# Probabilities applied in two runs of four steps, with eight places for their transposes

## The chip, the cores and the metric

The kernel runs on one core of a Trainium2 chip. The metric is the device time of one execution in microseconds (us). The kernel before took 1561.91 us, the median of 3 runs (1559.69 to 1562.31).

## What is computed

64 graphs of 128 nodes with 512 features go through two layers. The first is attention with 16 heads of 32 features; the adjacency matrix of the graph, taken twice, is added to the scores. The second is a graph convolution with one expert out of four for each graph, and a normalization over all the rows of an expert. Cut to the part that the change touches:

```python
h = maximum(layernorm(x), 0)
q, k, v = heads(h @ Wq.T), heads(h @ Wk.T), heads(h @ Wv.T)
a = einsum('bhnd,bhmd->bhnm', q, k) * 512 ** -0.5 + (adj + adj)
p = softmax(a)                                  # rows that are all zero give 0
o = einsum('bhnm,bhmd->bhnd', p, v)
x = x + merge(o) @ Wo.T
# then the expert layer on x
```

## The kernel before, in words

`attention_layer` works on pairs of graphs, 32 pairs in all. A pair has eight steps (`STEPS`): steps 0 to 3 are the four groups of four heads of its first graph, steps 4 to 7 those of its second. One step is a chain over all the engines, and each link is a letter in the order strings:

- `S` (TensorE, line 420): four score matmuls, one for each head, into one of two PSUM places.
- `L` (VectorE, 356 and 361): scaling and adjacency into `logits`, then the row maxima. `B` (364) tells all-zero rows, `R` (369, 372) makes the factor of each row.
- `E` (ScalarE, 301): four exponentials. `P` (GpSimd, 268): the probabilities times the row factor.
- `T` (TensorE, 427): four transposes of 128x128 into one of two PSUM places (`probT_ps`). `C` (ScalarE, 308) copies them to `probT` in SBUF.
- `W` (TensorE, 436): the probabilities are applied. It is a matmul for each of four heads, with 32 columns of `v` as weights and 128 columns of `probT` moving; each writes 32 partitions of `o_ps` (128 partitions, one 128-column place for each group of heads). In the trace each is two load and matmul pairs, so a `W` is eight loads and eight matmuls.

Beside the chain run the projections, each a sum of products of split operands by `exact_product` (line 43): `Q` 0 to 3 (24 matmuls each, the projections to queries and keys), `V` 0 and 1 (12 each), `O` 0 and 1 (12 each, the output projection), and `H` 0 and 1 (line 477, four transposes of the input). ScalarE and VectorE take each result out of PSUM as a high and a low part (`Q` at 319 and 387, `H` at 333 and 405, `O` at 312 and 377); ScalarE alone copies `V` (325). `X` on VectorE (381) adds the residual.

The order is written out by hand, one string for each engine, with one line for each step of the loop over pairs; each engine works its tokens strictly in this order. A prime means the pair before. Each token waits on semaphores, which count steps. The ones that matter here:

- `T` waits for the scaled probabilities of its step and for the copy `C` two steps before. `C` waits for the `W` that last read its place of `probT`.
- `W` waits for the copy of its step; `W0` and `W4` wait also for the copy of `v` and for the split of `o_ps` as it was before.
- `O` on ScalarE waits for the fourth `W` of its graph. `V` on ScalarE waits likewise, since it overwrites `v`.
- `Q2` on TensorE waits for the copy `V1'` (they share a bank).
- `K0` and `K1` on SyncE stack the split queries and keys for a graph's four steps: twelve DMAs each (line 249), issued one after the other. `K0` waits for the split of `Q3`, and `K1'` comes behind it on the queue with a store and a load in between. `S0` waits for `K0`'s data and `S4` for `K1'`'s; ScalarE's `Q0`, which overwrites what the copies read, waits for both.

The orders of ScalarE and GpSimd, which the change leaves alone:

```python
    ACT_ORDER = """H1' C6' E0
                   C7' E1
                   C0 Q0 O1' E2
                   V1' Q1 C1 E3
                   Q2 C2 E4
                   Q3 C3 E5
                   C4 A0 O0 E6
                   A1 V0 C5 H0 E7"""
    POOL_ORDER = "P7' D1' P0 P1 P2 P3 G P4 D0 P5 P6"
```

`probT` is also one of three tensors through which the raw weights are loaded at the start (`raw_weights`, 2048 values in each partition).

Of the kernel before, what the change touches and what calls it, by code (L numbers as in the profile page):

```python
# [25 lines left out]
ACT = mybir.ActivationFunctionType  # L26
# [6 lines left out]
def wait(engine, semaphore, value):  # L33

    if not isinstance(value, int) or value > 0:
        engine.wait_ge(semaphore, value)
# [31 lines left out]
def attention_layer(nc, ctx, sem, ident, x, adj, weights, x1_dram, expert_w, shared):  # L68
    w_hi, w_raw, w_raw_loaded, ew_hi_ready, ew_split, x1_in, x1_loaded = shared
    B, N, D = x.shape  # L70
    PAIRS = B // 2
    KC = D // 128
    R = 4
    C = HEADS // R
    HD = D // HEADS
    STEPS = 2 * C
    SCALE = float(D) ** -0.5
    STACKS = 16 * 3 * R

    def sb(name, shape, dt=F32):  # L80
        return ctx.enter_context(nc.sbuf_tensor(name, shape, dt))

    def ps(name, shape):
        return ctx.enter_context(nc.psum_tensor(name, shape, F32))
# [10 lines left out]
    v = sb("v", [N, 2, D])  # L95
    logits = sb("logits", [N, 4, R, N])
    prob = sb("prob", [N, 4, R, N])
    probT = sb("probT", [N, 4, R, N])
    o_hi = sb("o_hi", [128, C, N], F32R)
    o_lo = sb("o_lo", [128, C, N], F32R)  # L100
    x_res = sb("x_res", [N, 2, D])
# [18 lines left out]
    probT_ps = ps("probT_ps", [N, 2, R, N])  # L120
    o_ps = ps("o_ps", [128, C, N])
# [15 lines left out]
    transposed, probT_ready, applied = sem("transposed"), sem("probT_ready"), sem("applied")  # L137
# [8 lines left out]

    PE_ORDER = """S0 W5' T6' H1' O0'
                  S1 T7' W6' Q0  # L150
                  S2 T0 W7' Q1
                  S3 T1 W0 Q2
                  S4 W1 T2 Q3
                  S5 T3 W2 O1'
                  S6 T4 W3 V0
                  S7 T5 W4 H0 V1"""

    ACT_ORDER = """H1' C6' E0
                   C7' E1
# [31 lines left out]
    def tokens(engine, order, i):  # L191

        for t in (START.get((engine, i), order) if isinstance(i, int) else order).split():
            pair = 0 if t[0] in "UF" else i + (AHEAD[engine].get(t[0], 0) - t.endswith("'"))
            if not isinstance(pair, int) or 0 <= pair < PAIRS:
                yield t[0], int(t[1:].strip("'") or 0), pair

    def raw_weights(n):

        return (logits, prob, probT)[n % 3][:].rearrange("p k r n -> p k (r n)")  # L200

    def exists(pair):
        return not isinstance(pair, int) or pair < PAIRS
# [1 line left out]
    def run(engine, body):  # L205
        for i in (-2, -1, 0, 1):
            body(i)
        with engine.Fori(2, PAIRS - 2) as i:
            body(i)
        for i in (PAIRS - 2, PAIRS - 1, PAIRS):  # L210
            body(i)

    with nc.Block() as block:
# [70 lines left out]
        @block.scalar  # L284
        def _(act):
            def body(i):
                for token, k, j in tokens("act", ACT_ORDER, i):
                    slot = k % 4
                    if token == "U":
                        act.wait_ge(w_loaded[k], 16)  # L290
                        nc.scalar.activation(w_hi[:, k], raw_weights(k), ACT.Copy).then_inc(w_hi_ready, 1)
                    elif token == "F":
                        act.wait_ge(qk_projected, 4 * PAIRS)
                        act.wait_ge(v_projected, 2 * PAIRS)
                        act.wait_ge(w_raw_loaded[k], 16)
                        nc.scalar.activation(w_hi[:, k], w_raw[:, k].bitcast(F32), ACT.Copy).then_inc(ew_hi_ready, 1)
                    elif token == "E":
                        wait(act, neg_max_ready, STEPS * j + k + 1)
                        wait(act, transposed, STEPS * j + k - 3)
                        for r in range(R):  # L300
                            last = nc.scalar.activation(prob[:, slot, r], logits[:, slot, r], ACT.Exp,  # L301
                                                        bias=neg_max[:, slot, r:r + 1],
                                                        accum_out=row_sum[:, slot, r:r + 1])
                        last.then_inc(exp_done, 1)
                    elif token == "C":
                        wait(act, transposed, STEPS * j + k + 1)
                        wait(act, applied, STEPS * j + k - 3)
                        nc.scalar.activation(probT[:, slot], probT_ps[:, k % 2], ACT.Copy).then_inc(probT_ready, 1)  # L308
                    elif token == "O":
                        wait(act, applied, STEPS * j + C * (k + 1))  # L310
                        wait(act, o_projected, 2 * j + k)
                        nc.scalar.activation(o_hi[:], o_ps[:], ACT.Copy).then_inc(o_hi_ready, 1)
                    elif token == "Q":
                        wait(act, qk_projected, 4 * j + k + 1)
                        if k == 0:
                            for g in range(2):
                                wait(act, stacked[g], STACKS * j)
                        t, c = (Q_HI, K_HI)[k // 2], 2 * (k % 2)
                        nc.scalar.activation(qk[:, t, :, c:c + 2].rearrange("p g c n -> p c g n"),  # L319
                                             bank[:, Q_BANK[k]].rearrange("p (c g n) -> p c g n", c=2, g=2),  # L320
                                             ACT.Copy).then_inc(qk_hi_ready, 1)
                    elif token == "V":
                        wait(act, v_projected, 2 * j + k + 1)
                        wait(act, applied, STEPS * (j - 1) + C * (k + 1))
                        nc.scalar.activation(v[:, k], bank[:, V_BANK[k]], ACT.Copy).then_inc(v_copied, 1)
                    elif token == "A":
                        wait(act, shift_ready, j + 1)
                        wait(act, h_transposed, 2 * (j - 1) + k + 1)
                        nc.scalar.activation(h[:, k], x_in[:, k], ACT.Relu, bias=shift[:, k:k + 1],
                                             scale=rstd[:, k:k + 1]).then_inc(h_ready, 1)  # L330
                    elif token == "H":
                        wait(act, h_transposed, 2 * j + k + 1)
                        nc.scalar.activation(hT_hi[:, :, k], bank[:, H_BANK[k]].rearrange("p (c n) -> p c n", n=N),
                                             ACT.Copy).then_inc(hT_hi_ready, 1)

            run(act, body)

        @block.vector
# [72 lines left out]
        def _(pe):  # L411
            def body(i):
                for token, k, j in tokens("pe", PE_ORDER, i):
                    g, c, slot = k // C, k % C, k % 4
                    if token == "S":
                        if c == 0:
                            wait(pe, stacked[g], STACKS * (j + 1))
                        wait(pe, logits_ready, STEPS * j + k - 1)
                        for r in range(R):
                            last = nc.tensor.matmul(scores_ps[:, k % 2, r], stack[:, g, r, 0, c], stack[:, g, r, 1, c],  # L420
                                                    start=True, stop=True)
                        last.then_inc(scored, 1)
                    elif token == "T":
                        wait(pe, normed, STEPS * j + k + 1)
                        wait(pe, probT_ready, STEPS * j + k - 1)
                        for r in range(R):
                            last = nc.tensor.transpose(probT_ps[:, k % 2, r], prob[:, slot, r], ident[:])  # L427
                        last.then_inc(transposed, 1)
                    elif token == "W":
# [3 lines left out]
                            wait(pe, o_split, 2 * j + g)  # L433
                        for r in range(R):
                            f = HD * (R * c + r)
                            last = nc.tensor.matmul(o_ps[HD * r:HD * r + HD, c], v[:, g, f:f + HD], probT[:, slot, r],  # L436
                                                    start=True, stop=True)
                        last.then_inc(applied, 1)
                    elif token == "O":
# [11 lines left out]
                    elif token == "Q":  # L451
# [5 lines left out]
                        for half in range(2):  # L457
                            m = 128 * (2 * (k % 2) + half)
                            last = exact_product(nc, bank[:, Q_BANK[k], 256 * half:256 * half + 256],
                                                 [w_hi[:, k // 2, kc, m:m + 128] for kc in range(KC)],  # L460
                                                 [w_lo[:, k // 2, kc, m:m + 128] for kc in range(KC)],
                                                 [hT_hi[:, kc] for kc in range(KC)], [hT_lo[:, kc] for kc in range(KC)])
# [9 lines left out]
                    elif token == "H":  # L472
# [3 lines left out]
                        for kc in range(KC):  # L476
                            last = nc.tensor.transpose(bank[:, H_BANK[k], 128 * kc:128 * kc + 128],
                                                       h[:, k, 128 * kc:128 * kc + 128], ident[:])
                        last.then_inc(h_transposed, 1)

            keep_clock_up(nc, pe, bank[:, 0, 0:128], ident, 40)
            run(pe, body)


def expert_layer(nc, ctx, sem, ident, x1_dram, adj, router_w, router_b, gamma, beta, out_dram, y, shared):
# [92 lines left out]

    PE_ORDER = "Z0 Z1 J P0 P1 Z2 P2 Z3 P3 M"
    ACT_ORDER = "A2' A3' Z0 P0 A0 A1 Z1 P1 Z2 P2 Z3 P3"  # L580
# [66 lines left out]
    with nc.Block() as block:  # L647
# [255 lines left out]
        def _(pe):  # L903
            def body(i, stays):
                for token, g, group in tokens("pe", PE_ORDER, i):
                    n = G * group + g
# [146 lines left out]
```

## Time and profile before

| | |
|---|---|
| median of 3 runs | 1561.91 us |
| the profiled execution | 1559.98 us, span 1557.9 us |
| mean granted clock of TensorE | 0.977 of full speed |
| TensorE matmul busy | 1480.9 us (95%) |
| VectorE busy | 1137.4 us (73%) |
| ScalarE busy | 999.9 us (64%) |
| GpSimd busy | 444.7 us (29%) |
| attention layer | from the start to about 1140 us of the span |

Matmuls are pipelined: a matmul's record is some 0.28 us long, and the next one starts long before it has ended. So what a block of matmuls costs is read from the starts, from the first matmul of one block to the first or second matmul of the next, not from the durations. In the timeline, neighbours of one kind are merged to one row with a count.

### The profile page before, as it was taken

The page shows a single profiled execution, that of the slowest core. Times are in us where ns is not written, and L with a number is a line of the kernel's source. Part 1 is how long each engine was busy: PE and PEld are TensorE (multiplying, and loading weights), DVE is VectorE, ACT ScalarE, POOL GpSimd, SP SyncE. Part 2 cuts the span into 40 slices and gives each one's busy share as a digit, 9 for nine tenths or more (in the row PEclk, how much of TensorE's full clock was granted, in tenths as well). Part 3 has the DMA queues.
Part 4 walks back from the last instruction along what each step waited for, and adds up shares of the span by engine and source line. Part 5 has one row for each costly group of instructions (what it writes and reads, how often), then busy time and mean ns, then how long its engine had stood idle before and what let it go on. Part 6 is the DMA issues. An engine that isn't in the chain of part 4 may idle for free. (4 is left out here: it accounts for less than half of the span.)

```text
span 1557.9 us, 39084 instructions
## 1 busy us (share of the span) xinstructions
PE 1480.9 (95%) x11474; PEld 1264.9 (81%) x11475; DVE 1137.4 (73%) x2641; ACT 999.9 (64%) x3145; POOL 444.7 (29%) x529
## 2 busy tenths in 40 slices
PE   7999999999999999999999999999969999998885
PEld 6888888888888888888888888888757777777775
DVE  4777777777777777777777777777676667676685
ACT  4667666766676677666666766676644454453495
POOL 0223222322223222222232222222223343443200
PEclk9999999999999999999999999999879999999997
DMA  5965556666655566665555666654524332220798
GB/s 180 254 145 142 125 125 144 150 151 152 144 131 125 128 148 147 155 148 145 126 125 135 148 150 151 149 139 112 136 89 135 123 124 87 67 68 14 268 406 327
DMA packets 142135, 230.37 MB, mean 148 GB/s; under 512 B 17666, under 2 KB 34050, under 8 KB 142082
## 3 DMA queue, kind: packets, MB, share of 16 engines
q1 hardware_dynamic: 133634, 212.95, 52.7%
q10 hardware_dynamic: 8448, 16.78, 2.8%
q8 instruction: 25, 0.41, 0.1%
q14 instruction: 28, 0.23, 0.0%
HBM read 89.15 MB, written 39.85 MB: 83 GB/s over the span
## 5 line engine op out<-in xcount | busy, mean ns | idle before, releaser
L268 POOL TENSOR_TENSOR prob<-prob,norm 128x512 f32<-128x512 f32 x256 | 266.3, 1040 | 789.3 <-DVE norm L372 789.3
L301 ACT ACTIVATE prob<-logits,neg_max 128x128 f32<-128x128 f32 x1024 | 398.1, 394 | 69.7 <-DVE neg_max L361 69.6
L43 PE MATMUL bank<-hT_hi,w_hi 128*128 128x256 f32 x1024 | 303.1, 296 | 2.5 <-DVE hT_lo L405 2.2
L43 PE MATMUL bank<-hT_lo,w_hi 128*128 128x256 f32 x1024 | 290.7, 284 | 0.0
L43 PE MATMUL bank<-hT_hi,w_lo 128*128 128x256 f32 x1024 | 290.6, 284 | 0.0
L356 DVE SCALAR_TENSOR_TENSOR logits<-scores_ps,adj 128x512 f32<-128x512 f32 x256 | 176.7, 690 | 134.1 <-PE scores_ps L420 133.6
L308 ACT ACTIVATE probT<-probT_ps 128x512 f32<-128x512 f32 x256 | 152.7, 596 | 143.2 <-PE probT_ps L427 143.2
L43 PEld LDWEIGHTS bank<-hT_hi,w_hi 128*128 128x128 f32 x1024 | 196.7, 192 | 21.2 <-issue 19.5
L43 PEld LDWEIGHTS bank<-hT_lo,w_hi 128*128 128x128 f32 x1024 | 197.3, 193 | 0.0
L43 PEld LDWEIGHTS bank<-hT_hi,w_lo 128*128 128x128 f32 x1024 | 196.9, 192 | 0.0
L301 ACT ACTIVATION_READ_ACCUMULATOR prob<-logits,neg_max 128x1 f32 x1024 | 195.7, 191 | 0.0
L361 DVE TENSOR_REDUCE neg_max<-logits 128x4 f32<-128x512 f32 x256 | 175.7, 686 | 8.7
L364 DVE TENSOR_REDUCE abs_max<-logits 128x4 f32<-128x512 f32 x256 | 173.0, 676 | 0.0
L427 PE MATMUL probT_ps<-ident,prob 128*128 128x128 f32 x1024 | 163.6, 283 | 4.5 <-POOL prob L268 4.3
L420 PEld LDWEIGHTS scores_ps<-stack 96*128 96x128 f32 x1024 | 146.5, 193 | 16.4 <-DMA stack<-qk 5.6
L420 PE MATMUL scores_ps<-stack 96*128 96x128 f32 x1024 | 145.4, 265 | 4.7 <-DMA stack<-qk 4.7
L43 PE MATMUL out_ps<-w_hi,z_hi 128*128 x256 | 107.1, 418 | 20.6 <-issue 12.4
L750 ACT ACTIVATE z_hi<-z_ps 128x512 fp32r<-128x512 f32 x64 | 38.1, 598 | 137.4 <-PE out_ps L43 133.4
L427 PEld LDWEIGHTS probT_ps<-ident,prob 128*128 128x128 f32 x1024 | 108.6, 142 | 18.3 <-issue 12.7
L436 PE MATMUL o_ps<-probT,v 128*32 128x128 f32 x2048 | 109.8, 286 | 0.8 <-ACT probT L308 0.3
L387 DVE TENSOR_TENSOR qk<-bank,qk 128x512 fp32r<-128x512 f32 x128 | 87.8, 686 | 30.9 <-ACT qk L319 30.9
L319 ACT ACTIVATE qk<-bank 128x512 fp32r<-128x512 f32 x128 | 76.4, 597 | 52.4 <-PE bank L43 49.5
(138 smaller groups left out, 2921.5 us busy)
## 6 DMA issues: line engine op xcount, KB each, us to landing
stack<-qk SPq DMA_DIRECT2D x768, 128.0 KB, 2.5
x_in<-in_x SPq DMA_DIRECT2D x32, 512.0 KB, 4.7
x_res<-in_x SPq DMA_DIRECT2D x64, 256.0 KB, 2.9
x_dram<-x_res SPq DMA_DIRECT2D x64, 256.0 KB, 3.0
x_in<-x_dram SPq DMA_DIRECT2D x32, 512.0 KB, 3.7
y<-outs ACTq DMA_DIRECT2D x16, 1024.0 KB, 11.8
w_hi<-x_dram SPq DMA_DIRECT2D x8, 1024.0 KB, 17.9
out_dram<-outs SPq DMA_DIRECT2D x24, 256.0 KB, 2.0
```

What stands on the lines that cost most here:

```text
L43: last = nc.tensor.matmul(out, a, b, start=(n == 0), stop=(n == len(terms) - 1))
L268: nc.gpsimd.tensor_tensor(prob[:, slot], prob[:, slot], norm[:, slot].unsqueeze(2).to_broadcast([N, R, N]), ALU.mult).then_inc(normed, 1)
L301: last = nc.scalar.activation(prob[:, slot, r], logits[:, slot, r], ACT.Exp, bias=neg_max[:, slot, r:r + 1], accum_out=row_sum[:, slot, r: ...
L308: nc.scalar.activation(probT[:, slot], probT_ps[:, k % 2], ACT.Copy).then_inc(probT_ready, 1)
L319: nc.scalar.activation(qk[:, t, :, c:c + 2].rearrange("p g c n -> p c g n"), bank[:, Q_BANK[k]].rearrange("p (c g n) -> p c g n", c=2, g=2 ...
L356: nc.vector.scalar_tensor_tensor(out=logits[:, slot], in0=scores_ps[:, k % 2], scalar=SCALE, in1=adj2[:, k // C].unsqueeze(1).to_broadcast ...
L361: nc.vector.tensor_reduce(neg_max[:, slot], logits[:, slot], X, ALU.max, negate=True).then_inc(neg_max_ready, 1)
L364: nc.vector.tensor_reduce(abs_max[:, slot], logits[:, slot], X, ALU.max, apply_absolute_value=True).then_inc(abs_max_ready, 1)
L387: nc.vector.tensor_tensor(qk[:, lo, :, c:c + 2].rearrange("p g c n -> p c g n"), bank[:, Q_BANK[k]].rearrange("p (c g n) -> p c g n", c=2, ...
L420: last = nc.tensor.matmul(scores_ps[:, k % 2, r], stack[:, g, r, 0, c], stack[:, g, r, 1, c], start=True, stop=True)
L427: last = nc.tensor.transpose(probT_ps[:, k % 2, r], prob[:, slot, r], ident[:])
L436: last = nc.tensor.matmul(o_ps[HD * r:HD * r + HD, c], v[:, g, f:f + HD], probT[:, slot, r], start=True, stop=True)
```

## The change

The eight `W` tokens of a pair stood alone, one in each line of TensorE's order. Now four stand one behind the other in two places: `W0` to `W3` behind `T4`, and `W4'` to `W7'` of the pair before behind `T0`. The transposes wait longer before they are read, so `probT` has eight places in place of four, and the copy `C` waits for the `W` of eight steps before.

```diff
+    PROBT_SLOTS = 8
...
-    probT = sb("probT", [N, 4, R, N])
+    probT = sb("probT", [N, PROBT_SLOTS, R, N])
...
-    PE_ORDER = """S0 W5' T6' H1' O0'
-                  S1 T7' W6' Q0
-                  S2 T0 W7' Q1
-                  S3 T1 W0 Q2
-                  S4 W1 T2 Q3
-                  S5 T3 W2 O1'
-                  S6 T4 W3 V0
-                  S7 T5 W4 H0 V1"""
+    PE_ORDER = """S0 T6' H1' O0'
+                  S1 T7' Q0
+                  S2 T0 W4' W5' W6' W7' Q1
+                  S3 T1 Q2
+                  S4 T2 Q3
+                  S5 T3 O1'
+                  S6 T4 W0 W1 W2 W3 V0
+                  S7 T5 H0 V1"""
...
-        return (logits, prob, probT)[n % 3][:].rearrange("p k r n -> p k (r n)")
+        return (logits, prob, probT)[n % 3][:, 0:4].rearrange("p k r n -> p k (r n)")
...
                         wait(act, transposed, STEPS * j + k + 1)
-                        wait(act, applied, STEPS * j + k - 3)
-                        nc.scalar.activation(probT[:, slot], probT_ps[:, k % 2], ACT.Copy).then_inc(probT_ready, 1)
+                        wait(act, applied, STEPS * j + k - PROBT_SLOTS + 1)
+                        nc.scalar.activation(probT[:, k % PROBT_SLOTS], probT_ps[:, k % 2], ACT.Copy).then_inc(probT_ready, 1)
...
-                            last = nc.tensor.matmul(o_ps[HD * r:HD * r + HD, c], v[:, g, f:f + HD], probT[:, slot, r],
+                            last = nc.tensor.matmul(o_ps[HD * r:HD * r + HD, c], v[:, g, f:f + HD], probT[:, k % PROBT_SLOTS, r],
```

## Rows read from the trace of the kernel before

**Rows 1.** Windows: the middle pairs, the last pair; busy us of each engine, clock.
```profile
71.60:1106.00 1034.40, 1034.09 (x8397) 891.16 (x8398) 787.17 (x1760) 718.37 (x2517) 295.59 (x359) 1.00 0.60 141
1106.00:1145.00 39.00, 30.53 (x209) 22.40 (x207) 25.71 (x49) 24.19 (x80) 9.67 (x10) 0.82 0.36 106
```

**Rows 2.** Waits of TensorE's matmuls, 71.6 to 1106 us: total, times, longest.
```profile
PE scores_ps L420 <- DMA stack<-qk: 1.5, 1, 1.5
PE bank L43 <- ACT v L325: 0.3, 1, 0.3
```

**Rows 3.** Timeline of TensorE, three steps: start us, us, what, count.
```profile
503.11 0.56 PE L420 MATMUL scores_ps<-stack 96*128 96x128 f32 x4
...
503.96 0.66 PE L427 MATMUL probT_ps<-ident,prob 128*128 128x128 f32 x4
...
504.57 0.28 PE L43 MATMUL bank<-hT_lo,w_hi 128*128 128x256 f32 x1
...
520.24 0.56 PE L420 MATMUL scores_ps<-stack 96*128 96x128 f32 x4
520.72 0.43 PE L436 MATMUL o_ps<-probT,v 128*32 128x128 f32 x8
521.08 0.66 PE L427 MATMUL probT_ps<-ident,prob 128*128 128x128 f32 x4
521.58 0.60 PE L477 MATMUL bank<-ident,x_in 128*128 128x128 f32 x4
...
522.25 0.39 PE L43 MATMUL bank<-w_lo,o_hi 128*128 128x512 f32 x1
...
524.77 0.56 PE L420 MATMUL scores_ps<-stack 96*128 96x128 f32 x4
525.16 0.62 PE L427 MATMUL probT_ps<-ident,prob 128*128 128x128 f32 x4
525.72 0.43 PE L436 MATMUL o_ps<-probT,v 128*32 128x128 f32 x8
526.07 0.38 PE L43 MATMUL bank<-hT_hi,w_hi 128*128 128x256 f32 x1
526.30 0.28 PE L43 MATMUL bank<-hT_lo,w_hi 128*128 128x256 f32 x1
526.41 0.28 PE L43 MATMUL bank<-hT_hi,w_lo 128*128 128x256 f32 x1
```

**Rows 4.** Timeline: the weight loads of the `W` at 525.72.
```profile
525.72 0.16 PEld L436 LDWEIGHTS o_ps<-probT,v 128*32 128x32 f32 x8 [0.17 <-issue]
```

**Rows 5.** Timeline of TensorE: a block of small matmuls in the expert layer.
```profile
1201.28 0.95 PE L931 MATMUL router_ps<-rw,mean_h 128*1 128x4 f32 x32
```

**Rows 6.** Timeline: GpSimd's `P1` and TensorE's `T1`.
```profile
531.50 1.04 POOL L268 TENSOR_TENSOR prob<-prob,norm 128x512 f32<-128x512 f32 x1 [5.14 <-DVE norm L372]
...
533.71 0.62 PE L427 MATMUL probT_ps<-ident,prob 128*128 128x128 f32 x4
```

**Rows 7.** Timeline of SyncE's queue: issues of `K0`, then of `K1'`.
```profile
508.97 7.67 SPq L249 DMA_DIRECT2D stack<-qk  x12
...
518.44 7.67 SPq L249 DMA_DIRECT2D stack<-qk  x12
```

**Rows 8.** Line 249: issue to landing, of the second twelve of Rows 7.
```profile
DMA to landing us min/median/max: 3.9/4.1/4.2
```

**Rows 9.** The same, of all of line 249 from 100 to 1100 us.
```profile
DMA to landing us min/median/max: 2.3/2.5/5.6
```

**Rows 10.** Timeline: ScalarE's `Q0` and `V1'`, TensorE's `Q2`.
```profile
530.59 0.59 ACT L319 ACTIVATE qk<-bank 128x512 fp32r<-128x512 f32 x1
...
533.09 0.59 ACT L325 ACTIVATE v<-bank 128x512 f32<-128x512 f32 x1
...
534.62 0.38 PE L43 MATMUL bank<-hT_hi,w_hi 128*128 128x256 f32 x1
```

**Rows 11.** Waits of ScalarE, 71.6 to 1106 us: total, times, longest.
```profile
ACT qk L319 <- DMA stack<-qk: 2.5, 3, 1.2
```

## The prediction

> **What bounds the kernel now.** I read the page's busy shares and the slices of the granted clock first: TensorE is at 95% of the span, the next engine at 73%. Busy shares of pipelined matmuls flatter the engine, so I then asked for windows. From the first `S` of the second pair (71.6 us) to the first `S` of the last (1106.0 us) TensorE's matmuls are busy for 1034.09 of 1034.40 us, with the clock at 1.00, its level of 2.4 GHz [rows 1]. That is 30 pairs (8397 matmuls at 280 a pair), 34.48 us each. In the same stretch the table of waits gives the matmuls two waits for others, 1.8 us together [rows 2]. VectorE is busy for 76% of it and ScalarE for 69%. So in these 30 pairs TensorE's own order sets the time, and what is saved on it is saved in full until some other chain comes up.
>
> The third view is TensorE's timeline, which shows where its time goes without idling. Ahead of a `W` and behind it there are holes between starts. In a block of ordinary matmuls 0.11 us lies between starts (526.30 to 526.41). The eight matmuls of a `W` start close together (0.43 us from first start to last end, for records of 0.28 us), yet the transposes before take 0.56 us until the `W` starts, and the next block starts 0.35 us behind the `W`'s start [rows 3]. Its loads are over after 0.16 us, and the load side sat idle for 0.17 us before them for nothing that the profile names ("issue") [rows 4]. I read this as TensorE running empty each time it goes between matmuls over 128 columns of weights and matmuls over 32.
>
> **What a `W` costs now.** I measure from the first matmul of `S` to the second matmul of the projection (the first starts early and waits for its load). All from [rows 3]:
> - `S T W Q`: 526.30 - 524.77 = 1.53 us.
> - `S W T Q`: 504.57 - 503.11 = 1.46 us.
> - Without a `W`: `S` to `T` is 0.39 us (524.77 to 525.16); `T` to the second matmul of `Q` is 504.57 - 503.96 = 0.61 us, less 0.04, since a `T` behind a `W` runs 0.66 us and one behind an `S` 0.62 us. Sum 0.96 us.
> - So a `W` between `T` and a projection costs 0.57 us, and one between `S` and `T` 0.50 us.
> - `S W T H O`: 522.25 - 520.24 = 2.01 us; without the `W` 0.39 + (0.50 - 0.04) + 0.67 = 1.52 us, so 0.49 us.
>
> The starts are rounded to 0.01 us, so I take 0.56 for the five `W` ahead of a projection (`W6'`, `W7'`, `W0`, `W2`, `W3`) and 0.50 for the three between `S` or `T` and transposes (`W5'`, `W1`, `W4`). Sum for a pair: 2.80 + 1.50 = 4.30 us.
>
> **What it costs afterwards.** Two runs of four, each between `T` and a projection. The first `W` of each pays 0.56 us, which holds both emptyings. The other six pay what a `W` adds inside such a run, m. No two `W` stand together in the steady part, so m is bounded:
> - From below: a block of 32 load and matmul pairs of four columns runs 0.95 us from first start to last end with records of 0.17 us, so 0.025 us a pair [rows 5]; eight of them are 0.20 us.
> - From above: a `W` that empties the engine again for itself, 0.35 us from its start to that of the next block (525.72 to 526.07) [rows 3].
> - My value: the eight matmuls are two passes of four that run side by side. Four transposes with the same 128 moving columns take 0.62 us with records of 0.28 us, so 0.11 us each [rows 3]; two passes are 0.22 us. The single `W` supports it: 0.43 - 0.28 = 0.15 us from its first start to its last, of which a part is the first load.
>
> Then a pair's `W` cost 2 x 0.56 + 6 x 0.22 = 2.44 us, and 4.30 - 2.44 = 1.86 us are saved. Over 30 pairs: 55.8 us. With m = 0.20 it is 59 us; with m = 0.35 it is 1.08 us a pair, 32 us.
>
> **What the freed time runs into.** The step chains. `T1` and `T5` are the tight ones: `P1` ends at 532.54 and `T1` starts at 533.71, 1.17 us of cover [rows 6]. But between `S2`, on which `P1` hangs through VectorE's order, and `T1` three more `W` come in (+0.66 us), so this cover grows, and that of `T5` with it. All other transposes have no such `L` between their exponentials and their row factor and a cover over twice as long; they lose at most two `W`, 1.06 us. ScalarE's `O0` and `O1'` wait for the fourth `W`, which now ends 0.66 us later behind its `T`; but one copy and another operation (0.6 us and more each) stand ahead of them in ScalarE's order, so this costs 0.1 us there at most. The eight places cost nothing: `C` waits for a `W` that is long done, as before.
>
> The chain that does come closer is that of the stacking copies. `K0` starts when `Q3` is split, and `K0` and `K1'` keep SyncE's queue until 526.11; the last DMA is issued at 525.5 and takes 4.1 us to land [rows 7, 8], so it is there at 529.6. ScalarE's `Q0` starts at 530.59 [rows 10]: 1.0 us of cover. Between `Q3` and `Q0`'s place TensorE saves `W2`, `W4`, `W5'`, `W6'` (0.56 + 0.50 + 0.50 + 0.56) and gets three more in line 7 (0.66): 1.46 us. So `Q0` on ScalarE will wait some 0.5 us for the landing, in nearly each pair. Behind it in the order come `O1'`, `E2` and `V1'`, and TensorE's `Q2` waits for `V1'`: it ends at 533.68, `Q2` starts at 534.62, 0.94 us of cover [rows 10], and `Q2` itself moves by + 0.66 - 0.56 = 0.10 us. Cover together 1.0 + 1.04 against 1.46: 0.6 us are left, and TensorE doesn't feel it. In three of the 30 pairs `Q0` waited for the landing already, 2.5 us together [rows 11], and once the wait got through to TensorE [rows 2]. There the cover at `Q0` is nil: 3 x (1.46 - 1.04) + 2.5 = 3.8 us come back as stalls. I take 4 us, between nothing and, were it so in each pair with the longest landing (5.6 us [rows 9], 1.5 more than here), 30 x 0.9 = 27 us.
>
> **The ends.** The last pair and its tail have TensorE busy for 30.53 of 39.00 us, at a mean clock of 0.82 [rows 1]: it waits for the step chain there, which the change doesn't shorten. Only the first lines gain, 1 us or so. In the first pair the same: two `W` less ahead of `Q3` bring `K0` forward by up to 1 us. I take 2 us for both, of 0 to 3. The expert layer isn't touched.
>
> **Sum.** -55.8 + 4 - 2 = -53.8 us. Against the profiled execution (span 1557.9, in all 1559.98 us) that is 1506.2 us; the median of the runs lies 1.9 us above it, so 1508 us.
>
> **A rule that speaks against it.** In the trace 32 load and matmul pairs run at 0.025 us each [rows 5] and the eight matmuls of a `W` start within 0.15 us, 0.02 us each [rows 3]. The Trainium skill, "TensorE: Matmul & The Clock Gate", section "Wait — 56ns, not 53.3ns?", has the sequencer spend about 62 ns on each matmul when hardware decode is off, and names that as the bound for short matmuls. By that rule a `W` in a run would take at least 0.50 us by the page's figure, and the sum would be 1562 - 30 x 0.18 - 2 = 1555 us. These rows contradict it, unless a queue filled beforehand fed them; the rival "the run starves" is that doubt, with its price from rows.
>
> A second rule: the loads of a `W` are all issued while its own first matmuls run (loads over at 0.16 us, matmuls at 0.43 us [rows 3, 4]). The same page, section "The mechanism" of its Part 3, says that a load overlaps with matmuls in flight only when it goes to another row group, and all of these use all rows. By it each pass would wait out the one before. The trace of a single `W` disagrees, but has one change of weights only; the rival "no overlap" is this rule's.
>
> **The rivals.**
> - *Each `W` still empties the engine*, because each has its own waits and weights: m = 0.35, 1.08 us saved a pair, -32 - 2 and no stalls of the copies: 1528 us. For it: "issue" idling isn't explained by a semaphore. Against: the scores also wait token by token, and start 0.39 us ahead of the transposes with no hole [rows 3].
> - *The copies take over*: landing gets slower as the same DMAs fall in less time, and the chain `K0`, `K1'`, `Q0`, `V1'`, `Q2` sets the pair. At half of the upper bound above, 14 us, come back on top of my 4: 1522 us. For it: already three waits [rows 11] and a landing that varies from 2.3 to 5.6 us [rows 9].
> - *No overlap of loads in a run*: a pass takes its load (0.11 us) and its matmuls (0.15 us), m = 0.52; 4.30 - 1.12 - 3.12 = 0.06 us a pair: about 1560 us, no change.
> - *Slower: the run starves.* 64 loads and matmuls stand in a row. If those beyond what is queued come only as fast as the projections show them, 0.11 us a pair [rows 3], a `W` takes 0.88 us: 1.12 + 6 x 0.88 = 6.40 us a pair against 4.30, +63 us: 1625 us. It decides from m = (4.30 - 1.12) / 6 = 0.53 us, 0.066 us for a load and its matmul. For it: nothing shows that projections aren't fed at just that rate. Against: the 32 pairs at 0.025 us [rows 5].
>
> **How the numbers follow.** Forecast 0.66; copies take over 0.16; each `W` empties 0.09; no overlap 0.04; starves 0.04; 0.01 for something else. The first three are faster by far more than 0.2% (3 us, about what a measurement of this kernel tells from no change): faster 0.92 with part of the fourth, same 0.03, slower 0.05. The forecast's own range is 1502 (m = 0.20, no stalls) to 1517 (m = 0.26). The range reaches on to the copies' and to the emptying case: 1501 to 1530.
>
> **What would show it.** In the profile after: a pair of 32.6 to 32.8 us; a merged row of 32 matmuls of line 436, 1.1 us long (0.28 + 0.15 + 3 x 0.22), longer in the rivals (1.5 emptying, 2.0 no overlap, 3.1 starving); "issue" idling ahead of line 436 down to a quarter; ScalarE's `Q0` waiting for the stacking DMAs in most pairs, 0.3 to 1 us each; TensorE's waits for `V` a few us in all; `T1` and `T5` with more cover than before. I am wrong if TensorE shows waits of over 10 us for others between 71.6 us and the last pair, or if the run of 32 is over 1.4 us long.

## The result and the profile after

The changed kernel took 1517.62 us, the median of 4 runs (1513.03 to 1519.4), against 1561.11 us for the one before on the same chip: a ratio of 0.9717, with a 95% interval from 0.9692 to 0.9743. The forecast was 1508 us, with a range from 1501 to 1530. The profiled execution took 1519.4 us, its span was 1517.6 us. On a second chip the changed kernel took 1507.55 us; what lies between the two is taken up below.

First the run of four `W` in TensorE's timeline, in a stretch where nothing disturbs it. The columns are start, duration, what, and count; PEld is the side that loads weights.

```profile
744.28 0.56 PE L421 MATMUL scores_ps<-stack 96*128 96x128 f32 x4
744.68 0.62 PE L428 MATMUL probT_ps<-ident,prob 128*128 128x128 f32 x4
745.24 1.08 PE L437 MATMUL o_ps<-probT,v 128*32 128x128 f32 x32
...
749.62 0.62 PE L428 MATMUL probT_ps<-ident,prob 128*128 128x128 f32 x4
750.00 0.36 PE L43 MATMUL bank<-hT_hi,w_hi 128*128 128x256 f32 x1
...
776.97 0.56 PE L421 MATMUL scores_ps<-stack 96*128 96x128 f32 x4
```

```profile
745.23 0.81 PEld L437 LDWEIGHTS o_ps<-probT,v 128*32 128x32 f32 x32 [0.17 <-issue]
...
746.24 0.19 PEld L43 LDWEIGHTS bank<-hT_hi,w_hi 128*128 128x128 f32 x1 [0.20 <-issue]
```

The 32 matmuls take 1.08 us where eight took 0.43 [rows 3]: (1.08 - 0.43) / 3 = 0.22 us for each further `W`. The hole of 0.17 us ahead of the loads [rows 4] and the one of 0.20 us behind them are there once for a run. The two `S` at 744.28 and 776.97 are one pair apart: 32.69 us, where the 30 pairs before took 34.48 each (an undisturbed one 34.47).

Now the middle pairs, from the second pair's first `S` to the last pair's, and the last pair (columns as in rows 1):

```profile
70.90:1064.10 993.20, 985.96 (x8396) 900.72 (x8397) 786.42 (x1758) 724.53 (x2517) 296.29 (x358) 1.00 0.62 146
1064.10:1105.00 40.90, 28.86 (x218) 23.23 (x216) 27.27 (x52) 24.26 (x82) 9.91 (x12) 0.83 0.36 106
```

They take 993.2 us in place of 1034.4 [rows 1], which is 41.2 us less; the span is only 40.3 us shorter, since the last pair and what follows it take longer. But 30 undisturbed pairs would take 30 x 32.69 = 980.7 us. The other 12.5 us are stalls, and they are not spread evenly: the first two of the 30 pairs (first `S` at 70.90, 105.92 and 143.23 us) take 35.02 and 37.31 us, which is 7.0 us of it. TensorE's waits from 71 us on, where rows 2 had 1.8 us, and ScalarE's that goes with it (rows 11 had 2.5 us, 3 times); total, times, longest:

```profile
PE bank L43 <- ACT v L326: 6.7, 7, 2.8
PE scores_ps L421 <- DMA stack<-qk: 2.4, 2, 2.0
```

```profile
ACT qk L320 <- DMA stack<-qk: 21.4, 21, 3.2
```

The longest one, step by step. First the landings of the twelve DMAs of `K1'` issued between 105.5 and 113.5 us (rows 8 had 4.1 in the middle), then ScalarE, then TensorE:

```profile
DMA to landing us min/median/max: 4.6/4.9/6.5
```

```profile
119.39 0.60 ACT L320 ACTIVATE qk<-bank 128x512 fp32r<-128x512 f32 x1 [3.17 <-DMA stack<-qk]
...
121.90 0.58 ACT L326 ACTIVATE v<-bank 128x512 f32<-128x512 f32 x1
```

```profile
122.53 0.54 PE L43 MATMUL bank<-hT_hi,w_hi 128*128 128x256 f32 x1 [2.75 <-ACT v L326]
122.87 0.42 PE L43 MATMUL bank<-hT_lo,w_hi 128*128 128x256 f32 x1
123.08 0.41 PE L43 MATMUL bank<-hT_hi,w_lo 128*128 128x256 f32 x1
```

`Q0` waits 3.17 us for the landing, `V1'` comes 2.5 us behind it, `Q2` comes on its heels. And the wait costs more than itself: behind it the matmuls start 0.21 us apart and not 0.12. The windows show the granted clock, the third number from the end, there, behind the wait of 1.98 us at 70.9 us, and in an undisturbed stretch:

```profile
70.90:74.40 3.50, 3.50 (x15) 3.21 (x16) 1.78 (x3) 1.04 (x3) 1.12 (x2) 0.57 1.05 275
122.50:126.00 3.50, 3.46 (x16) 3.47 (x17) 3.27 (x13) 2.61 (x10) 1.03 (x1) 0.52 0.10 39
744.30:747.80 3.50, 3.50 (x55) 3.13 (x54) 2.54 (x7) 2.11 (x8) 1.04 (x1) 1.00 0.85 219
```

Behind the idle stretches of 2.0 and 2.75 us the clock was at its lower level of 1.2 GHz for most of the 3.5 us that follow, in which about half the work is done: 0.43 and 0.48 of 3.5 us, some 1.6 us lost each time. Of the 12.5 us, then, 7.1 are waits in the table (without the 1.98 us, which end where the stretch begins) and some 3 are the clock. The rest is overlap that is lost, some 0.25 us at each of the eight waits: undisturbed, the projection starts 0.38 us behind `T` (749.62 to 750.00), while `T`'s record of 0.62 us still runs, and the table counts a wait only from the end of that record.

### The profile page after: what moved, and what is told of

It reads as the page before. It is cut to its first block and busy times, and to the rows that moved or that the text cites. A ratio compares the mean times of both kernels' runs of the same rounds, so it can differ in the third digit from the quotient of the medians.

```text
span 1517.6 us, 39024 instructions
## 1 busy us (share of the span) xinstructions
PE 1427.6 (94%) x11474; PEld 1273.3 (84%) x11475; DVE 1136.7 (75%) x2641; ACT 1005.8 (66%) x3145; POOL 445.7 (29%) x529
## 5 line engine op out<-in xcount | busy, mean ns | idle before, releaser
L43 PE MATMUL bank<-w_hi,o_hi 128*128 128x512 f32 x256 | 108.3, 423 | 1.4 <-DVE o_lo L378 1.4
L43 PE MATMUL bank<-w_hi,hT_hi 128*128 128x512 f32 x256 | 106.4, 416 | 1.5 <-DVE qk L388 1.5
```

Of the source, the lines that this page charges most:

```text
L43: last = nc.tensor.matmul(out, a, b, start=(n == 0), stop=(n == len(terms) - 1))
```

## The experiments

All ratios are to the kernel before on the chip of the experiment, where it took between 1559.5 and 1560.6 us.

**The places alone.** `PROBT_SLOTS = 8` with TensorE's old order.

```diff
+    PROBT_SLOTS = 8
...
     PE_ORDER = """S0 W5' T6' H1' O0'
                   S1 T7' W6' Q0
```

> The eight places of probT alone, TensorE's order as before. My theory (all of the change in time comes from where the W stand): 1561 us, no change, pairs of 34.48 us. Rival (the places matter, since copies no longer wait for a W): a few us faster.

Measured: 1559.47 us, ratio 0.9992 (0.9983 to 1.0002), and TensorE's waits between the second pair and the last are empty. The places do nothing by themselves; all that follows is order.

**One graph at a time.** First only `W0` to `W3` stand together, then only `W4'` to `W7'`, both with the eight places. The order against that of the kernel before, in excerpts:

```diff
                   S2 T0 W7' Q1
-                  S3 T1 W0 Q2
-                  S4 W1 T2 Q3
-                  S5 T3 W2 O1'
-                  S6 T4 W3 V0
+                  S3 T1 Q2
+                  S4 T2 Q3
+                  S5 T3 O1'
+                  S6 T4 W0 W1 W2 W3 V0
```

> Only W0 to W3 stand together, behind T4; W4' to W7' stand alone as before. My theory: three W no longer empty the engine for themselves, and a W in a run adds 0.22 us, so a pair takes 34.48 - (2 x 0.56 + 0.50 - 0.66) = 33.5 us, some 29 us in 30 pairs, and Q0 on ScalarE keeps its lead on the stacking copies (it loses W2, 0.56, and gains 0.66), so hardly any stalls: 1532 us, TensorE waits under 3 us in the middle pairs. Rival (what the changed kernel lost against my sum is spread over both runs of four, whatever the copies do): half of what the changed kernel gained, 1539 us.

```diff
-    PE_ORDER = """S0 W5' T6' H1' O0'
-                  S1 T7' W6' Q0
-                  S2 T0 W7' Q1
+    PE_ORDER = """S0 T6' H1' O0'
+                  S1 T7' Q0
+                  S2 T0 W4' W5' W6' W7' Q1
...
-                  S7 T5 W4 H0 V1"""
+                  S7 T5 H0 V1"""
```

> Only W4' to W7' stand together, behind T0; W0 to W3 alone as before. My theory: 2 x 0.50 + 0.56 - 0.66 = 0.90 us saved a pair, 27 us. Q0 on ScalarE comes 1.56 us earlier against the copies than before, and so waits for the landing in most pairs; but Q2 comes 0.66 us later behind T0, so the cover is 1.0 + 1.6 us and the stalls are fewer than in the changed kernel: 1536 us, with the first pairs losing some us while the expert weights are loaded. Rival: half of what the changed kernel gained, 1539 us, with no wait for the copies.

Measured: 1532.12 us (0.9824, 0.9804 to 0.9844) and 1536.44 us (0.9844, 0.9827 to 0.9862). The waits of TensorE and of ScalarE's `Q0`, the first graph's kernel above, the second's below:

```profile
PE bank L43 <- ACT v L326: 1.1, 1, 1.1
...
ACT qk L320 <- DMA stack<-qk: 1.5, 1, 1.5
```

```profile
PE o_ps L437 <- DVE o_lo L378: 1.6, 1, 1.6
PE scores_ps L421 <- DMA stack<-qk: 0.9, 1, 0.9
PE bank L43 <- ACT v L326: 0.7, 1, 0.7
...
ACT qk L320 <- DMA stack<-qk: 12.2, 21, 3.5
```

The two savings, 27.9 and 23.6 us, add up to 51.5 us, where both together gave 43.5 on the first chip and 52.0 on the second (below). TensorE's own part adds up exactly: an undisturbed pair takes 33.52 us with the first graph's run and 33.64 with the second's, 0.95 and 0.83 us less than 34.47, and with both 32.69, 1.78 less. What is missing on the first chip are stalls, and they belong to neither run of four alone. With the second graph's, `Q0` waits for the copies in 21 cases, but TensorE hardly feels it, since `Q2` comes 0.66 us later in that order. It feels it in one pair, 2.3 us in all, where the late `Q0` also held up `O1'` and with it `W0` (the wait for `o_lo`). Only with both runs is the cover used up.

**`V1'` ahead of `Q0`.** The changed kernel with another order on ScalarE:

```diff
-                   C0 Q0 O1' E2
-                   V1' Q1 C1 E3
+                   C0 O1' V1' Q0 E2
+                   Q1 C1 E3
```

> The changed kernel with ScalarE's order turned from 'C0 Q0 O1' E2 V1' Q1' to 'C0 O1' V1' Q0 E2 Q1', so that V1', for which TensorE's Q2 waits, no longer stands behind Q0, which waits for the landing of the stacking copies. My theory (TensorE's lost time is this chain: landing, Q0, O1', E2, V1', Q2): the waits for V go and 8 to 12 us come back, 1506 us, and runs of it differ by less than the 6 us that runs of the changed kernel differ. Rival (the copies' ring as such sets the pair, by way of S0, S4 or the exponentials E2): no change, 1517 us, and TensorE waits for something else instead.

Measured: 1506.83 us (1505.96 to 1512.46), ratio 0.9667 (0.9642 to 0.9693). The waits for `V` are gone; all that TensorE waits between 71 and 1050 us is

```profile
PE scores_ps L421 <- DMA stack<-qk: 0.4, 1, 0.4
```

That is 7.8 us less than the changed kernel by the ratios, whose intervals just touch. The spread came out as large as before (one run of 1512.46), so that part of the expectation isn't borne out. And the landings were another matter too: the longest from 100 to 1050 us was 5.4 us here and 6.5 us in the changed kernel's profiled execution, so the order and kinder landings aren't told apart by this run. I took this for the confirmation; the later runs made it smaller.

**A smaller load ahead of the copies.** The load of the next input before `K1'` brings only 64 of 512 columns, and the kernel leaves out the rest, so what it computes is not the reference's result; ScalarE keeps the order of the changed kernel.

```diff
-                        sp.dma_start(x_in[:], x[bass.ds(2 * j, 2)].rearrange("g n f -> n g f")).then_inc(x_loaded, 16)
+                        sp.dma_start(x_in[:, :, 0:64], x[bass.ds(2 * j, 2)].rearrange("g n f -> n g f")[:, :, 0:64]).then_inc(x_loaded, 16)
```

> The changed kernel, but of each 512 KB load of the next input that stands on SyncE's queue right before the stacking copies K1' only an eighth of the columns is loaded (64 of 512; the rest of the place keeps old values, so the output isn't the reference's). ScalarE's order is that of the changed kernel. My theory (K1' lands late, 4 us after its issue and not 2.5, since its packets share the DMA engines with this load, and that lateness is what reaches TensorE by way of Q0 and V1'): K1' lands up to 1.5 us sooner, waits for V are gone in the middle pairs, about 1507 us. Rival (the lateness comes from the copies themselves): no change, 1517 us.

Measured: 1504.29 us, ratio 0.9644 (0.9628 to 0.966). All landings of line 250 from 100 to 1050 us, this kernel, then the changed one (100 to 1060 us):

```profile
DMA to landing us min/median/max: 2.3/2.4/3.9
```

```profile
DMA to landing us min/median/max: 2.3/2.5/6.5
```

ScalarE's `Q0` waits for no copy any more and TensorE for nobody between 71 and 1050 us. So the late landing is the load's doing: it is issued right before `K1'`, and with an eighth of it `K1'` lands early. The landings show this; the time is clear of the first chip's for the changed kernel, but its interval touches the second chip's (below).

**A wide `W`.** What makes the holes? Here each `W` takes 128 columns of `v`, so that its matmuls have the width of all the others. Its heads overwrite each other in `o_ps`, so the result isn't the reference's. One kernel has the runs of four, the other the old order.

```diff
-                            last = nc.tensor.matmul(o_ps[HD * r:HD * r + HD, c], v[:, g, f:f + HD], probT[:, k % PROBT_SLOTS, r],
+                            last = nc.tensor.matmul(o_ps[:, c], v[:, g, 128 * c:128 * c + 128], probT[:, k % PROBT_SLOTS, r],
```

> The changed kernel, but each matmul of a W takes 128 columns of v as weights and writes all 128 partitions of o_ps, in place of 32 columns and 32 partitions (the four heads of a step overwrite each other, so the output isn't the reference's). My theory (TensorE runs empty where it goes between matmuls over 128 and over 32 columns of weights): the holes ahead of and behind the runs are gone, the first W starts 0.11 us behind the last transpose and not 0.20, but the eight matmuls of a W come one after the other at 0.11 us, 0.88 us a W: a pair takes 34.48 - 4.30 + 8 x 0.88 = 37.2 us, 1640 us in all. Rival (the holes come from the wait for the copy or from going to another kind of block): holes of 0.20 us stay on both sides, and a pair takes 37.8 us.

> The same wide W, but each alone in TensorE's order as before the change. My theory: without the change of width there is nothing to save by standing together, so a pair takes the same 37.2 us as in the kernel with runs of four and wide W, 1642 us. Rival (the emptying hangs on the waits or on the kind of block): eight separate W pay it eight times, 37.2 + 8 x 0.3 = 39.6 us a pair, 70 us slower than the runs of four.

Measured once each: 1652.28 and 1648.95 us. The timelines, first with the runs of four, then with each `W` alone:

```profile
528.44 0.62 PE L428 MATMUL probT_ps<-ident,prob 128*128 128x128 f32 x4
528.90 3.74 PE L437 MATMUL o_ps<-probT,v 128*128 128x128 f32 x32
532.39 0.36 PE L43 MATMUL bank<-hT_hi,w_hi 128*128 128x256 f32 x1
...
752.60 0.56 PE L421 MATMUL scores_ps<-stack 96*128 96x128 f32 x4
...
790.03 0.56 PE L421 MATMUL scores_ps<-stack 96*128 96x128 f32 x4
```

```profile
536.85 0.62 PE L428 MATMUL probT_ps<-ident,prob 128*128 128x128 f32 x4
537.31 1.06 PE L437 MATMUL o_ps<-probT,v 128*128 128x128 f32 x8
538.12 0.36 PE L43 MATMUL bank<-hT_hi,w_hi 128*128 128x256 f32 x1
...
752.08 0.56 PE L421 MATMUL scores_ps<-stack 96*128 96x128 f32 x4
...
789.56 0.56 PE L421 MATMUL scores_ps<-stack 96*128 96x128 f32 x4
```

`T` to `W` is now 0.46 us with or without a run, where the narrow `W` stood 0.56 us behind [rows 3], and the projection follows with no hole. A pair takes 37.43 us with the runs and 37.48 us without; that the whole kernel with the runs took 3.3 us longer comes from behind these pairs, in one execution each. With one width there is nothing to save by standing together: waits, tokens and kinds of block are the same in both, so the holes are the change of width (and of the part of `o_ps` that is written, which changes with it). That wide `W` are dearer all the same (0.87 us against 0.56) is the four heads going one after the other.

**Both orders again, side by side on another chip.** The changed kernel and the one with `V1'` ahead, five executions each.

> The changed kernel again, beside the one with V1' ahead of Q0, on one chip. My theory (its losses are landings of the copies that come late by chance): 1512 to 1520 us, with a spread of some 6 us between executions and 5 to 9 waits of TensorE for V in the profiled one, 4 to 9 us in all.

> The changed kernel with V1' ahead of Q0 in ScalarE's order again. My theory: 1505 to 1508 us, some 8 to 11 us under the changed kernel beside it, and no wait of TensorE for V between the second pair and the last. Rival (the difference of the first look was one of chips): both the same.

Measured: 1507.55 us (1504.34 to 1509.89; ratio 0.9672, 0.9658 to 0.9685) and 1504.77 us (1503.0 to 1509.41; 0.9656, 0.9643 to 0.9669). My expectation for the changed kernel was wrong: it lies 10 us below the first chip's. Its waits, TensorE's and ScalarE's, and its landings from 100 to 1050 us:

```profile
PE bank L43 <- ACT v L326: 0.3, 1, 0.3
```

```profile
ACT qk L320 <- DMA stack<-qk: 6.6, 17, 1.3
```

```profile
DMA to landing us min/median/max: 2.3/2.5/4.3
```

Here the longest landing is 4.3 us where it was 6.5, `Q0` waits 6.6 us in all where it was 21.4, and the cover behind it swallows nearly all of that: the same 30 pairs take 980.8 us. So the order of the changed kernel is as good as the landings that it meets; the other order's gain here, 2.8 us, has overlapping intervals and isn't shown.

**The landing made late.** One more load of 512 KB right before `K1'`, to a place in DRAM that nothing reads, with both orders of ScalarE. The diff shows the load alone.

```diff
                         sp.dma_start(x_in[:], x[bass.ds(2 * j, 2)].rearrange("g n f -> n g f")).then_inc(x_loaded, 16)
+                        wait(sp, x_again_loaded, 16 * (j - 1))
+                        sp.dma_start(x_again, x[bass.ds(2 * j, 2)]).then_inc(x_again_loaded, 16)
```

> The changed kernel plus one more load of the next input right before K1' on SyncE's queue, 512 KB to a place in DRAM that nothing reads. It makes the landing of K1' late on purpose, by its issue (about 0.6 us) and by its packets (an eighth of the first such load in place of the whole brought the landing 1.5 us forward, so up to 1.5 us more). My theory (a late landing reaches TensorE by Q0, O1', E2, V1', Q2, with some 0.6 us of cover): 0.5 to 1.5 us lost in most pairs, 1525 to 1555 us, and TensorE waits for V in over 20 pairs. Rival (the waits for V in the first profile were chance of another kind): under 1512 us.

> The same additional load, with V1' ahead of Q0 in ScalarE's order. My theory: V1' no longer hangs on the landing, and Q0 and E2 have over 2 us of cover, so 1505 to 1515 us and no waits for V. Rival (the late copies reach TensorE also by E2 and the transposes, or by S4): as slow as with the order of the changed kernel.

Measured: 1555.49 us (0.9974, 0.9952 to 0.9995) with the changed kernel's order and 1545.3 us (0.9906, 0.9868 to 0.9943) with `V1'` ahead. TensorE's waits from 71 to 1090 us, in this order:

```profile
PE bank L43 <- ACT v L331: 35.0, 29, 2.4
PE scores_ps L426 <- DMA stack<-qk: 1.8, 1, 1.8
```

```profile
PE scores_ps L426 <- DMA stack<-qk: 19.9, 28, 2.1
PE probT_ps L433 <- POOL prob L274: 6.5, 14, 1.4
```

The chain by way of `V1'` is there in 29 pairs, as my theory has it, and one more load gives nearly all of the gain back, a little beyond my 1555 us. With `V1'` ahead these waits are gone, but my 1505 to 1515 us were wrong: the scores now wait for their copies in 28 cases. `Q0` stands in a ring: it waits for `K1'`, and the next `K0` waits for the split of `Q3`, which comes behind it. The order of `V1'` opens one way from the landing to TensorE, not the ring.

What carries the lateness from `Q0` to the next `K0` is VectorE's order, as one pair of the kernel with `V1'` ahead shows: ScalarE's `Q0`, VectorE's `Q0` and `Q3` (line 393), the issue of `K0`, and the first `S`:

```profile
694.40 0.60 ACT L325 ACTIVATE qk<-bank 128x512 fp32r<-128x512 f32 x1 [1.48 <-DMA stack<-qk]
```

```profile
695.03 0.69 DVE L393 TENSOR_TENSOR qk<-bank,qk 128x512 fp32r<-128x512 f32 x1 [3.01 <-ACT qk L325]
...
704.84 0.69 DVE L393 TENSOR_TENSOR qk<-bank,qk 128x512 fp32r<-128x512 f32 x1
```

```profile
705.65 7.67 SPq L254 DMA_DIRECT2D stack<-qk  x12
```

```profile
715.24 0.66 PE L426 MATMUL scores_ps<-stack 96*128 96x128 f32 x4 [0.53 <-DMA stack<-qk]
```

VectorE waits 3.01 us for ScalarE's `Q0`, and from there to its `Q3` it has so much other work in its order that it idles for 0.5 us only. It takes 10.5 us for this stretch here, and 10.5 us in the kernel with `V1'` ahead and no additional load too, so a late `Q0` reaches `K0`, and through its data `S0`, nearly undiminished. `R2`, on which `T2` hangs through `P2`, stands behind VectorE's `Q0` as well: these are the waits for `prob`.

## Why the prediction was right, and where it was off

*TensorE's order is the bound.* Right. The places alone change nothing, and undisturbed pairs are shorter by what TensorE's blocks are.

*A `W` costs 0.50 or 0.56 us, of which most is emptying; in a run 0.22 us.* Right: 0.22 us in the profile, and the wide `W` shows the change of width as the cause, which was a reading of holes before. The sum over a pair was 1.86 us, measured 34.48 - 32.69 = 1.79: 2 us too much over 30 pairs. It lies in the `W` that stood alone. I had put the paths without a `W` together from rows of other blocks, rounded to 0.01 us; line by line, before against the changed kernel, the eight come to 4.19 us and not 4.30 (0.54 to 0.57 ahead of a projection, 0.47 to 0.49 for the others).

*The two rules that spoke against it.* 32 loads took 0.81 us and 32 matmuls 1.08 us, 0.03 us each, the loads ending while matmuls ran. The Trainium skill, "TensorE: Matmul & The Clock Gate", section "Wait — 56ns, not 53.3ns?", has about 62 ns for each matmul with hardware decode off; by that figure the run would be 2 us long (an estimate from this figure of the Trainium skill). No run here shows which way this kernel's matmuls are decoded, only that 62 ns don't bind them. The same page of the Trainium skill, section "The mechanism" of its Part 3, has a load overlap with matmuls in flight only when it goes to another row group; these loads take all rows, and the measurement decides against it here.

*The copies' chain: 4 us.* The mechanism was right to the link (landing, `Q0`, `V1'`, `Q2`; 21 waits at `Q0`, seven at TensorE), the size was not: 12.5 us in the profiled execution. This is the term that was mis-sized, for two reasons. I took the landings of one execution on one chip as they stood, three of them late, and they vary: the longest is 5.6 us before [rows 9], 6.5 and 4.3 us in two executions of the same changed kernel, and with the short one the stalls are 0.6 us. And I priced a wait at its own length: of the 8.5 us beyond my 4, some 3 are the clock behind two waits and 2 the overlap that is lost at each. That the second chip's 1507.55 us are the forecast's number is partly luck: there the stalls are 3 us less than forecast and the `W` save 2 us less. Why landings differ stays open. The changed kernel's executions on the two chips don't overlap (1513.03 to 1519.4 us, and 1504.34 to 1509.89), which speaks for something that lasts on a chip or for a time rather than for chance in each execution; two chips don't settle it. My sign of being wrong, waits of over 10 us, was just missed: the table has 9.1 us, the stalls come to 12.5.

*The ends: 2 us.* Wrong in sign in this execution. The first pair brought 0.7 us (71.6 to 70.9), and from the last pair's first `S` to the end of the span it is 451.9 us before and 453.5 us after. But both ends vary by more than that from execution to execution: on the second chip the changed kernel has 70.2 and 451.6 us, and the kernel with the places alone, whose order is the old one, 70.3 and 451.4. So these traces tell nothing of what the change brings there.

Together: 53.8 forecast, less 2 for the `W`, 8.5 for the stalls and 3 for the ends, is 40.3 us, the difference of the two spans.

*The rivals.* The run of 32 of 1.08 us rules out emptying for each `W`, no overlap and starving. The copies taking over, with its 1522 us, was the nearest: on the first chip the kernel came two thirds of the way from 1508 to it, on the second nowhere, and far beyond it (1555.49 us) with the landing made later on purpose.

## What to carry over

Where TensorE is the bound, look for blocks of narrow matmuls (32 columns of weights) scattered among full ones: here each stay cost two holes, some 0.3 us in all (0.56 - 0.22), and making two stays of eight took 1.8 us from a pair of 34.5. Before shortening the bound engine's loop, write down for each transfer in it how far it lands ahead of its use and how much of that distance is the work that goes; take the longest landing of several executions for it, and expect that the clock may come on top of a wait of some 2 us. An operation that waits for a transfer belongs behind those that the bound engine waits for, as long as the engines behind it have slack for its lateness: with `V1'` ahead of `Q0` the kernel took 1506.83 and 1504.77 us, the least of those that leave nothing out; side by side with the changed kernel on one chip the 2.8 us between them aren't told from chance.

## What the hardware showed that I had not expected

After an idle stretch of 2.0 us TensorE's granted clock was down, at 0.57 over the next 3.5 us, in a kernel that had kept it busy before. Behind the wait of 1.3 us the clock stayed at 1.00:

```profile
422.08:425.58 3.50, 3.50 (x29) 3.50 (x30) 3.27 (x13) 2.90 (x11) 1.00 (x1) 1.00 0.11 42
```

But the length of the idle stretch doesn't settle it. In the kernel with the smaller load TensorE idled for 2.08 us at the same place, and the clock stayed up:

```profile
69.51 0.33 PE L421 MATMUL scores_ps<-stack 96*128 96x128 f32 x1 [2.08 <-DMA stack<-qk]
```

```profile
69.51:73.01 3.50, 3.50 (x22) 3.12 (x23) 2.65 (x5) 1.90 (x7) 1.02 (x2) 1.00 0.88 203
```

In the kernel with the additional load it stayed at 1.00 behind a wait of 2.22 us and fell to 0.68 behind one of 1.88 us. What decides between them no run here shows, so a wait of some 2 us may or may not cost the 1.6 us.

And a load of 512 KB ahead on the same queue moves the landing of all twelve DMAs behind it, while the median of all these copies hardly shows it. The `K1'` of one middle pair, in the changed kernel and with an eighth of the load:

```profile
DMA to landing us min/median/max: 3.9/4.1/4.1
```

```profile
DMA to landing us min/median/max: 2.3/2.3/2.4
```
